# Transposed score tiles issued head by head, each with its own filling tile, in a two-layer transformer kernel

## The reference, cut to what matters

```python
def _attn(x, W_qkv, b_qkv, W_out, b_out):
    ...
    scores = jnp.einsum('bnqd,bnkd->bnqk', q, k) * scale
    scores = jnp.where(causal, -jnp.inf, scores)
    attn = jax.nn.softmax(scores, axis=-1)
    out = jnp.einsum('bnqk,bnkd->bnqd', attn, v)
    ...

def _ffn(x, w_gate, w_up, w_down):
    return jnp.einsum('bsh,dh->bsd', _silu(gate) * up, w_down)

x = x + _attn_a(_layernorm(x)); x = x + _ffn(_layernorm(x))
x = x + _attn_b(_layernorm(x)); x = x + _ffn(_layernorm(x))
```

## Time and profile before

| | us |
|---|---|
| median of 3 runs | 2178.95 |
| lowest and highest run | 2174.32 and 2179.26 |
| the profiled execution | 2179.44 |
| its span | 2177.7 |
| PE busy | 2113.8 (97%) |
| PE weight loads busy | 1486.4 (68%) |
| DVE busy | 1253.6 (58%) |
| POOL, ACT busy | 668.9 (31%), 530.9 (24%) |
| mean granted clock of TensorE | 0.997 of 2.4 GHz |

### The profile page before, as it was taken

One profiled execution on the slowest core, in us unless ns is written; L12 is line 12 of the kernel. 1 busy time (PEld: TensorE's weight loads), 2 busy tenths in 40 slices (PEclk: granted clock), 3 DMA queues, 4 the chain that ended last, 5 costly groups with the idle time before them and its releaser, 6 DMA issues.

```text
span 2177.7 us, 34223 instructions
## 1 busy us (share of the span) xinstructions
PE 2113.8 (97%) x11056; PEld 1486.4 (68%) x11056; DVE 1253.6 (58%) x2476; ACT 530.9 (24%) x1076; POOL 668.9 (31%) x508
## 2 busy tenths in 40 slices
PE   6999999999999999999989999999999999999998
PEld 5555478888755548888865554888877554588886
DVE  6766564544676647444467665644456767454445
ACT  1344420000144441000014454100011444310001
POOL 3324233332312323323231233333323223233322
PEclk9999999999999999999999999999999999999999
DMA  4333111111323211111242321111113232111113
GB/s 130 94 79 79 31 36 52 49 58 39 79 70 79 70 31 49 50 48 49 68 129 70 79 69 40 39 59 39 49 40 81 68 81 68 40 49 49 59 39 97
DMA packets 59748, 135.15 MB, mean 62 GB/s; under 512 B 10784, under 2 KB 11808, under 8 KB 59552
## 3 DMA queue, kind: packets, MB, share of 16 engines
q1 hardware_dynamic: 59552, 132.71, 21.6%
HBM read 77.62 MB, written 4.19 MB: 38 GB/s over the span
## 4 chain that ended last, share of the span: by engine, by line
PE 88%; issue 5%; DVE 2%; POOL 2%; ACT 1%; DMA 1%; SPq 0%; DVEq 0%; POOLq 0%; ACTq 0%
PE ring L898 13%; PE ring L899 13%; PE ring L900 13%; PE bank L1011 13%; PE ring L965 8%; PE bank L989 7%; PE bank L898 7%; PE bank L900 7%; PE bank L899 7%; PE ring L889 1%; ACT prob L560 1%; DMA area<-nm_lo 1%; POOL area L438 1%; DVE xn L699 1%; POOL prob L463 1%
## 5 line engine op out<-in xcount | busy, mean ns | idle before, releaser
L898 PE MATMUL ring<-xt_hi,area 128*128 128x512 f32 x1248 | 489.8, 392 | 1.1 <-DVE kq_parts L688 1.1
L899 PE MATMUL ring<-xt_lo,area 128*128 128x512 f32 x1248 | 486.4, 390 | 0.0
L900 PE MATMUL ring<-xt_hi,area 128*128 128x512 f32 x1248 | 486.0, 389 | 0.0
L699 DVE CUSTOM_DVE_ANT_0 xn<-ring,mask_row 128x128 bf16<-128x128 f32 (+7 forms) x512 | 374.5, 749 | 99.9 <-PE ring L965 93.9
L560 ACT ACTIVATE prob<-bank 128x512 f32<-128x512 f32 (+3 forms) x768 | 335.0, 489 | 342.4 <-PE bank L989 341.6
L436 POOL TENSOR_SCALAR area<-w_stage 128x1024 fp32r<-128x1024 f32 x131 | 144.4, 1103 | 762.2 <-PE bank L900 404.7
L766 DVE TENSOR_TENSOR prob<-prob,ring 128x512 f32<-128x512 f32 x128 | 87.8, 686 | 456.9 <-ACT prob L578 456.9
L438 POOL TENSOR_TENSOR area<-w_stage,area 128x1024 fp32r<-128x1024 f32 x131 | 322.8, 2464 | 10.9
L578 ACT ACTIVATE prob<-ring 128x512 f32<-128x512 f32 x128 | 76.5, 598 | 970.4 <-PE ring L900 970.4
L898 PEld LDWEIGHTS ring<-xt_hi,area 128*128 128x128 f32 x1248 | 234.3, 188 | 59.1 <-issue 9.8
L900 PEld LDWEIGHTS ring<-xt_hi,area 128*128 128x128 f32 x1248 | 234.3, 188 | 49.1
(11 more groups left out here) (78 smaller groups left out, 2053.4 us busy)
## 6 DMA issues: line engine op xcount, KB each, us to landing
w_stage<-ffn_w SPq DMA_DIRECT2D x96, 512.0 KB, 3.3
area<-kq_parts SPq DMA_DIRECT2D x336, 128.0 KB, 2.4
w_stage<-attn_w SPq DMA_DIRECT2D x35, 512.0 KB, 3.3
x<-x_in SPq DMA_DIRECT2D x24, 256.0 KB, 3.9
area<-attn SPq DMA_DIRECT2D x48, 128.0 KB, 2.3
out<-x SPq DMA_DIRECT2D x16, 256.0 KB, 2.2
bias_rows<-row_bias SPq DMA_DIRECT2D x10, 256.0 KB, 4.2
area<-nm_hi SPq DMA_DIRECT2D x32, 8.0 KB, 1.8
```

The source lines that it names most:

```text
L699: dve.tensor_tensor_reduce(out=sum_out[:, RING[name] % 2, 0:keys], in0=src[:, 0:keys], in1=mask_row[:, TOKENS - keys:], scale=1.0, scalar= ...
L898: pe.matmul(dst, ah, bh, start=first and k == 0, stop=False)
L899: pe.matmul(dst, ah, bl, start=False, stop=False)
L900: ins = pe.matmul(dst, al, bh, start=False, stop=last and k == n - 1)
```

## The change

The four score tiles of a key tile are issued one by one, and each is followed by the filling tile of its own point. The values of key tile j-1 stand right behind score tile 1, the sums right behind score tile 3, each ahead of the filling tile of that point. So the order for a key tile is

1. score tile 0, filling tile of the first point,
2. score tile 1, values, filling tile of the second point,
3. score tile 2, filling tile of the third point,
4. score tile 3, sums, filling tile of the fourth point.

The points themselves stay. With it the copy at the end of `split_max` goes: the second half of the split hands the buffer back, and SP's transfers wait for that count.

```diff
+WEIGH_AFTER = {1: "values", 3: "sums"}
...
             def stack_max(it, u):
-                wait_alone(sp, max_split, it * UNITS + u + 1)
+                wait_alone(sp, ring_drained, drained(it, ("mt", u)))
...
                     dve.scalar_tensor_tensor(nm_lo[:, :], src, -1.0, nm_hi[:, :].bitcast(F32), ALU.mult,
-                                             ALU.subtract).then_inc(max_split, 1)
-
-                    dve.wait_ge(max_split, it * UNITS + u + 1)
-                    dve.tensor_copy(row_max[0:1, u % 2, 0:1], row_max[0:1, u % 2, 0:1]).then_inc(ring_drained, 1)
+                                             ALU.subtract).then_inc(ring_drained, 1)
...
                     for j in range(1, key_tiles(u)):
-                        for half, what in enumerate(("values", "sums")):
-                            for own in range(2):
-                                if own == 0:
-                                    scores_t(u, j, 2 * half)
-                                    scores_t(u, j, 2 * half + 1)
-                                else:
-                                    weigh(u, j - 1, what)
-                                for (name, *which), at in zip(beside(u)[early:], points(u)):
-                                    if at == point and (name != "mt" or which[0] not in MAX_LATE):
-                                        run[name](*which)
-                                point += 1
+                        for h in range(GH):
+                            scores_t(u, j, h)
+                            if h in WEIGH_AFTER:
+                                weigh(u, j - 1, WEIGH_AFTER[h])
+                            for (name, *which), at in zip(beside(u)[early:], points(u)):
+                                if at == point and (name != "mt" or which[0] not in MAX_LATE):
+                                    run[name](*which)
+                            point += 1
```

More of the change, by code:

```diff
@@ L232, in block_kernel @@
             sem("ring_drained"), sem("stats_done"), sem("var_ready"), sem("xn_ready"))
-        max_ready, nm_hi_done, max_split, recip_done = (
-            sem("max_ready"), sem("nm_hi_done"), sem("max_split"), sem("recip_done"))
+        nm_hi_done, recip_done = sem("nm_hi_done"), sem("recip_done")
         side_taken = sem("side_taken")
```

## The result

The changed kernel takes 2183.22 us (median of 10 runs, 2182.01 to 2184.64) against 2178.89 us for the kernel before on the same chip. The ratio is 1.0025 with a 95% interval from 1.0015 to 1.0035. It is slower, by some 4 to 5 us, and stays within 0.3%. One of the ten executions of the kernel before took 2339.2 us and does not enter the ratio. I had forecast 2181.4 us, in a range from 2174.5 to 2188: the sign is right, but the loss is about twice the 2.5 us of my sum.

A forecast was written before the change was run, and what follows sets the result against it. The prediction took PE, busy 2113.8 of 2177.7 us, as the bound. Its terms 0.15 + 0.35 + 0.30 - 0.17 gave +0.63 us a pass, +2.5 us for four, so a median of 2181.4 us, range 2174.5 to 2188.

The forecast's parts named there:

- Only small terms, no new bound: PE, busy 2113.8 of 2177.7 us, stays the bound; the change keeps the number of borders, so only small terms.
- The rival of the ring as bound: Odd units: more filling tiles wait for DVE's maxima, 11.9 us on top, 2193 us; chance 0.13, wholly or half.
- The mask did not pay in full: Rival, units 2, 4, 6: mask costs 0.47 us each instead of 0.10, 4.4 us on top, 2185.8 us; chance 0.07.
- Spreading helped: Faster rival, changed stretches: alternating order hides loads and all three copies count, 2174.8 us; chance 0.16.
- The load rule: Each of 220 changed stretches hides one more 128-column load, 0.107 us, 23 us in all, 2155 us; chance 0.02.
- DVE's waits, +0.35: Late filling tiles hold back a score tile: +0.17 us in unit 0, +0.06 in each odd unit, per pass.
- Borders, +0.15: New order inside stretches costs 0.01 us in each of 15 odd-unit stretches where a narrow filling tile stood last.
- The mask, +0.30: Units 2, 4, 6, key tile 2: score tile 3 is issued later, so mask and values come 0.10 us later each.
- The copy, -0.17: Buffer back about 0.17 us sooner without DVE's copy; gain booked in unit 3 only, -0.17 us a pass.
- The sum: All terms together: +0.63 us for a pass, +2.5 us for four passes.
- What would show it: Profile signs: odd-unit stretches 0.88 to 0.90 us, steps within 0.02 us, values 0.05 to 0.06 us after the mask.

The follow-up runs named there:

- short maxima: Kernel before and changed kernel, each with every DVE row maximum taken over the first 128 keys only: 2161.69 and 2166.59 us, one execution each.
- narrow_kept: Changed kernel, but a filling tile whose last product is 128 columns wide stays behind its pair of score tiles: 2182.3 us, one execution.
- mask_kept: Changed kernel, but in units 2, 4, 6, key tile 2, the third point's filling tile stays behind score tile 3: 2181.53 us, one execution.
- copy_only: Kernel before without the copy of line 716, PE's order untouched: 2179.49 us against 2179.11, ratio 0.9998.
- order_only: Changed kernel with the copy of line 716 put back, so only PE's order differs from the kernel before: 2182.74 us against 2179.11, ratio 1.0016.

## Why the prediction was right or wrong, point by point

- **Only small terms, no new bound.** Right. The rival of the ring as bound wanted waits for maxima in early key tiles with 3 x 0.33 us in an odd unit; no step of that kind is there, and only the tiles that I had named push others back. The mask did not pay in full (0.154 of 0.47 us). Spreading helped by some 0.05 us in five stretches of a pass, against a loss of 1.25 us by the order as a whole.
- **The load rule.** In sentences of its own I had weighed the rule of the Trainium skill (TensorE: Matmul & The Clock Gate, the bullets on what overlaps), by which each alternation would hide a load. It fell, and the trace disagrees with it: the ordinary stretch went from 0.88 to 0.89 us, and apart from the five stretches with two 128-wide score tiles, which gained some 0.05 us each, none gained more than some 0.02. Where a load shows, it shows behind a short product, whoever loads which rows.
- **DVE's waits, +0.35.** Right, at +0.17 in unit 0 and +0.05 net in each odd unit. The step ahead of the sums was +0.17 instead of the +0.11 that I wrote, since the score tile behind the narrow product brings a load that shows, 0.04 us with short maxima. Taking the narrow pair of key tile 7 apart gave 0.05 us back. That the two come out even is luck: neither stood in my sum. The two kernels with short maxima show that the rest was DVE.
- **Borders, +0.15.** This step failed, by its size. I had the right steps in hand, 0.28 us for the score tile behind a 128-wide product against 0.23, and still charged a flat 0.01 us for each of 15 stretches, half of a figure that I read as "within rounding". The four borders cost +0.02, +0.02, +0.045 and +0.02 us, 0.32 for a pass. The reading that "it holds where a narrow filling tile stood last" left out units 2 and 4, where a pair with a 128-wide product stands at key tile 0: +0.09. With the +0.02 of unit 0 this is 0.43 instead of 0.15, 1.1 us of the time. narrow_kept shows the part that hangs on the narrow product.
- **The mask, +0.30.** Mechanism right (0.06 us from the mask's end to the values, in all three units), size off: 0.154 instead of 0.10. The mis-sized term is the exponential. I took 0.33 us, half of a pair, and alone it takes 0.38. mask_kept shows that the step is the filling tile's place. It is 0.6 us of the time.
- **The copy, -0.17.** The mechanism failed, and the size came out by luck. I followed the chain from the copy over the reciprocals "to the load that waits" and left out POOL: DVE's multiplication in that chain ended 0.54 us after POOL's subtraction, whenever it began. In units 1 and 3 nothing is won. What the copy cost lies ahead of the first values of units 0 and 5, where I had booked nothing: -0.04 and -0.06 us in copy_only, -0.06 and -0.06 between order_only and the change. Through unit 6 its removal takes 0.08 us from a pass in the old order and 0.18 in the new one. I followed neither chain, and why the new order gains more is open.
- **The sum.** For the order alone I had 0.15 + 0.35 + 0.30 = 0.80 us, and order_only measures 1.25. The two misses, borders (+0.28) and mask (+0.16), make up the difference, and what the copy's removal takes back, 0.18, leaves 1.07. Both misses erred in the change's favour, and each by taking a mean where a single row gave the dearer figure.
- **What would show it.** The steps between score tile and filling tile held within 0.02 us, and the ordinary stretch too (0.89). That did not make the stretches equal: where 0.28 took the place of 0.23, one grew by 0.045. And two score tiles of 128 columns were in no row that I had read. In units 2, 4 and 6 I named the wrong tile: the values that start 0.06 us behind the mask are those of key tile 2, issued in the turn of key tile 3.

## What to carry to other kernels

When an order is changed inside a stretch that repeats, take the cost of every adjacent pair from a row of that very pair (here filling tile 128 wide before score tile: 0.28 instead of 0.23 us) and multiply by the count, since 0.02 to 0.05 us at 220 places are a good part of the effect. A load of 128 columns shows behind a 128-wide product: a tile that ends narrow lost when it was moved from `weigh` with its short loads to a score tile, and pairs of narrow score tiles won by being parted. Before booking a gain for an engine's chain, look at what the other engines run beside each link, and for the wait that would be late next. The holes worth filling were those that the timeline shows on PE itself, 0.4 to 0.6 us at three places of a pass, and not the ones with the large totals in the waits of the load side: with short maxima that total rose from 95.5 to 113.0 us while the kernel became 14.6 us faster.

## What the runs showed of the hardware that I had not expected

- DVE's multiplication of two operands in SBUF (128 x 512) takes 0.69 us with POOL idle and 1.06 to 1.27 us beside POOL's subtraction of 128 x 1024. Its end then hangs on POOL's, 0.54 to 0.55 us after it in four kernels (before, change, order_only and copy_only), and moving POOL's work away restores 0.69. The other way round it holds too: in unit 6 of the kernel before, POOL's mask starts at 775.23, 0.15 us into such a multiplication (775.08, 0.69 us), and takes 1.03 us instead of 0.64. The Trainium skill (SBUF — State Buffer, "SBUF: two separate sides") says that DVE and GpSimd share a port pair as an exclusive lock, also for a DVE operation with two SBUF inputs against a GpSimd operation that reads SBUF. This case agrees: the multiplication is held and not slowed in proportion, since an earlier start bought no earlier end. It ends 0.54 us and not its full 0.69 after POOL, so some 0.15 us of it pass while it is held.
- A weight load of 128 columns behind a product 128 wide shows by about 0.05 us (0.28 instead of 0.23 for the score tile); behind a product 256 wide the next start comes after 0.12 us, half of the 0.23 to 0.24 behind one 512 wide, so there it does not show.
- An exponential of 128 x 256 out of PSUM takes 0.38 us alone, and two in a row 0.66.
- Short stretches at half of TensorE's clock, none to four of them in an execution, add about 1.5 us each. The mean granted clocks of the runs bear it out: of 26 executions of the kernel before on one chip, the twelve at 0.996 took 2181.3 us in the mean and the nine at 0.998 or 0.999 took 2176.3. That is most of the scatter (2175.16 to 2182.0 us), and it is why differences below 0.2% were read from steps between named instructions.
